# A fused attention and feed-forward block on Trainium2: taking out the filler matmuls of the attention stage and issuing each diagonal chunk last

## What is computed

```python
xn = layernorm(x)
q, k, v = xn @ Wq.T, xn @ Wk.T, xn @ Wv.T        # 16, 16, 64 features per head
qf, kf = taylor_exp(q), taylor_exp(k)            # [1, x/2, (x outer x)/(sqrt(2)*4)]
A = tril(einsum('bhnd,bhmd->bhnm', qf, kf))
y = einsum('bhnm,bhme->bhne', A, v)
y = y * rsqrt(mean(y*y) + 1e-5) * g_weight       # per token and head
attn = y @ Wo.T
h = gelu(einsum('bsd,fd->bsf', xn, ternary(W1)) + b1)
ffn = einsum('bsf,df->bsd', h, ternary(W2)) + b2
out = x + attn + ffn
```

## Time and profile before

| what | us |
|---|---|
| median of 2 runs | 1793.25 (1790.44 and 1796.06) |
| profiled execution | 1789.8 |
| its span on the slowest core (core 4) | 1787.9 |
| spans of the eight cores | 1754.8 to 1787.9 |

### The profile page before, as it was taken

How to read it: one execution, slowest core, us unless ns; L and a number is a source line. 1 busy time by engine, 2 the same in 40 slices (tenths; PEclk the granted TensorE clock), 3 DMA queues, 4 the chain that set the end, 5 groups by cost and what they waited for, 6 DMA issues and landing times.

```text
span 1787.9 us, 16908 instructions; the slowest of 8 cores (1754.8 to 1787.9 us)
## 1 busy us (share of the span) xinstructions
PE 1266.6 (71%) x4584; PEld 438.1 (25%) x4584; DVE 569.5 (32%) x1295; ACT 532.9 (30%) x886; POOL 93.1 (5%) x155
## 2 busy tenths in 40 slices
PE   0000296798979797989978872937888881499996
PEld 0000043122222222212222221313333330244442
DVE  2222007644343444334354443443222220000100
ACT  1553332344333444324444432212233330000000
POOL 1111000000000000000000000001111110000000
PEclk9999698686555777656668685968999996699998
DMA  8889905000010101010001016844445446465662
GB/s 190 258 262 219 175 1 94 7 8 11 1 18 0 18 1 30 1 30 1 14 16 30 1 24 153 299 168 147 158 153 158 159 156 191 126 163 138 153 163 48
DMA packets 154328, 176.24 MB, mean 99 GB/s; under 512 B 73856, under 2 KB 125056, under 8 KB 150144
## 3 DMA queue, kind: packets, MB, share of 16 engines
q0 software_dynamic: 24928, 97.53, 19.7%
q1 hardware_dynamic: 129312, 77.63, 17.3%
HBM read 119.56 MB, written 41.94 MB: 90 GB/s over the span
## 4 chain that ended last, share of the span: by engine, by line
PE 49%; DMA 30%; DVE 10%; issue 6%; SPq 2%; ACT 1%; POOL 1%; DVEq 0%; POOLq 0%; ACTq 0%
PE psY L726 12%; PE psY L711 11%; DMA wst<-w2T 9%; PE psS L758 9%; PE psS L833 6%; DMA p1st<-w1T 5%; PE psS L705 4%; DMA xnT<-xn_tm 4%; DMA hg_ts<-hg_scr 4%; DMA w_sb<-w2t_scr 3%; PE psY L833 2%; DMA y_tm<-y_pair 2%; PE psS L797 2%; PE psY L797 2%; DVE jw2a L551 1%
## 5 line engine op out<-in xcount | busy, mean ns | idle before, releaser
L639 ACT ACTIVATE A_buf<-psS,consts 128x512 bf16<-128x512 f32 (+3 forms) x427 | 282.2, 711 | 456.5 <-PE psS L758 455.3
L758 PE MATMUL psS<-qh_ext,kh_ext 16*128 16x512 bf16 (+3 forms) x640 | 216.9, 427 | 109.9 <-DVE A_buf L460 83.4
L811 PE MATMUL psS<-xnT,w_sb 128*128 128x512 bf16 x1024 | 230.0, 383 | 76.9 <-DVE w_sb L515 39.4
L711 PE MATMUL psY<-v_tm,zlhs 128*128 128x512 bf16 x512 | 247.6, 484 | 0.0
L726 PE MATMUL psY<-A_buf,v_tm 128*64 128x512 bf16 (+3 forms) x640 | 235.4, 482 | 0.0
L456 DVE TENSOR_SCALAR pv<-psS 128x512 bf16<-128x512 f32 (+3 forms) x213 | 129.6, 608 | 261.1 <-PE psS L758 251.7
L705 PE MATMUL psS<-xnT,wq_bf 128*128 128x512 bf16 x64 | 21.2, 504 | 207.8 <-DMA xnT<-xn_tm 207.8
L833 PE MATMUL psS<-w_sb,hg_ts 128*128 128x512 bf16 x512 | 113.6, 383 | 64.6 <-DMA hg_ts<-hg_scr 64.4
L811 PEld LDWEIGHTS psS<-xnT,w_sb 128*128 128x128 bf16 x1024 | 98.3, 98 | 208.4 <-issue 98.3
L672 ACT ACTIVATE hgst<-psS,consts 128x512 bf16<-128x512 f32 x128 | 84.9, 685 | 178.5 <-DMA hg_scr<-hgst 108.5
L833 PE MATMUL psY<-w_sb,hg_ts 128*128 128x512 bf16 x512 | 111.8, 379 | 0.0
(11 more groups left out here) (96 smaller groups left out, 738.2 us busy)
## 6 DMA issues: line engine op xcount, KB each, us to landing
p1st<-w1T POOLq DMA_DIRECT2D x16, 1024.0 KB, 7.5
p1st<-w2T POOLq DMA_DIRECT2D x16, 1024.0 KB, 8.5
wst<-w1T POOLq DMA_DIRECT2D x16, 1024.0 KB, 8.4
wst<-w2T POOLq DMA_DIRECT2D x32, 512.0 KB, 4.8
hg_scr<-hgst SPq DMA_DIRECT2D x128, 128.0 KB, 2.7
hg_ts<-hg_scr SPq DMA_DIRECT2D x32, 512.0 KB, 7.8
x_roll<-x SPq DMA_DIRECT2D x16, 512.0 KB, 6.1
out<-out_sb SPq DMA_DIRECT2D x16, 512.0 KB, 5.0
```

Source lines behind the costliest of these rows:

```text
L639: e.activation(A_buf[:, gs % 4, t0:t0 + w], psS[idx % 4][:, 0:w], AF.Square, bias=cc(C_CBI), scale=cc(C_CSC)).then_inc(sPOLY, 1)
L711: e.matmul(psY[:, 1536:2048], zlhs[:], v_tm[:, 0, 0:512], start=False, stop=False)
L758: e.matmul(psS[idx % 4][:, 0:w], kh_ext[:, hi, m * 128:(m + 1) * 128], qh_ext[:, hi, t0:t0 + w], start=True, stop=True).then_inc(sSC, 1)
L811: mm = e.matmul(ps[:], w12_sb[:, c * FF + j * 128:c * FF + j * 128 + 128], xnT[:, 4 * tb:4 * tb + 4, c, :], start=(c == 0), stop=(c == KD ...
```

## The change

```diff
@@ -715,7 +715,9 @@
             chs = strip_chunks(m)
             for hi, h in ((0, 2 * p), (1, 2 * p + 1)):
                 gs = strip_of[(p, m, hi)]
-                for ci, (t0, w) in enumerate(chs):
+                order = list(range(1, len(chs))) + [0]
+                for ci in order:
+                    t0, w = chs[ci]
                     idx = poly_idx[(p, m, hi, ci)]
                     if ci == 0:
                         e.wait_ge(sDM, dm_of[(p, m, hi)] + 1)
@@ -728,7 +730,6 @@
                              A_buf[:, gs % 4, t0:t0 + w],
                              start=False, stop=False)
                 e.sem_inc(sAV, 1)
-                dummy_mm(e)
 
         def close_b(e, p, b):
```

## The result

The changed kernel takes 1594.0 us (median of 11 runs, 1584.4 to 1621.4). The kernel before, run beside it, takes 1789.0. The ratio is 0.893, with a 95% interval of 0.889 to 0.897: 10.7% faster. Medians and ranges here are of all runs; ratios and comparisons leave out runs such as the one of 1621.4, in which one die took longer at a lower clock.

What follows compares the result with a forecast made beforehand. TensorE was taken to bound the attention stage by its streaming and clock. 318.4 + 617 (pairs of 77.7) + 739.8, less 3.3 tail and 16 clock return, gave 1656; profiling and median offsets made 1661 us, range 1600 to 1710.

Steps and rivals of the forecast that it cites:

- The wait at a pair's head: TensorE's wait for the transpose and VectorE's normalizing: 9.2 us, plus 0.7 us without the first filler.
- the check: Attention stage: ScalarE and VectorE can keep up with 77.7 us a pair; four score buffers cover ScalarE's 0.7 us lag.
- The later stages: Everything after the last score, taken as untouched: 739.8 us carried over for core 6, expected to be slowest.
- The chunk order: Diagonal chunk last in AV strips: wins nothing where filler covered the mask, now a guard; put at 0.
- rival 3: Attention blocks: filler hid a wait for the mask before AV; 25 us a pair, 1880 us, slower; chance 0.04.
- A switch between scores and AV: Two per block stay, 32 a pair, at 0.13 us each: 4.2 us a pair (0 to 8).
- rival 2: Attention stage: only the filler's streaming comes free, each switch keeps its 0.25 us; 16 us a pair, 1771 us; chance 0.10.
- Rival 1: Blocks 5 to 12: the clock holds high, saving 12 us a pair; 1581, or 1595 with misses; chance 0.24.
- the sum: One attention pair at 1.2 GHz throughout: 61.4 + 4.2 + 9.2 + 0.7 + 2.2 = 77.7 us.
- streaming that stays: AV as many: Attention pair: scores 34,816 columns, AV as many, plus 8 matmuls of 512: 73,728 columns, 61.4 us.
- the return of the clock: Two clock lifts a pair after AV in blocks 0 to 3, about 1 us each: 16 us off the time.
- The wait at a pair's tail: After a pair's last score: of five fillers' 3.3 us only 1.1 comes off, 2.2 turns into waiting.

Runs made afterwards that it cites:

- experiment 1: Changed kernel with head 1's AV matmuls writing to the same 64 PSUM partitions as head 0's, no instruction added or removed: 1671.2 us, ratio to before 0.933.
- Experiments 1 and 2: The second: changed kernel plus one matmul of zeros, 128 wide and 16 columns long, between the two heads' AV strips: 1702.1 us, ratio 0.951.

## Why the prediction was right and where it failed

**Right.** TensorE sets the pace; the filler stood on its path; without it the clock stays low throughout (0.50 in the stage, the granted clock of every slice) and the kernel is faster all the same. The cores came closer, 25 us apart (1564.2 to 1588.9) instead of 33. The wait at a pair's head was 9.8 us in the mean of the eight on core 1 (7.2 to 11.2), where the account had 9.2 + 0.7. ScalarE and VectorE kept up as the check said: outside the heads of pairs the scores waited for VectorE 9.8 us in the whole stage, where it was 10.9 before, and no longer for ScalarE. The later stages were not changed by the edit, but they are not as steady as I took them: the slowest core was core 1, with 731.6 us, and core 6, which I had expected to be slowest with 739.8, needed 722.1 and was the fastest. The chunk order won nothing, and AV waits for the mask 5.7 us in all, which ends rival 3. A switch between scores and AV costs about what I took: in experiment 1 eight AV matmuls hold TensorE 3.55 us for 3.41 of streaming, 0.14 for 0.13 taken, so rival 2 is gone as well. Rival 1, the clock held in the middle blocks, named nearly the right time (1595) by luck, for a wrong reason: no block of the stage ran at the higher level.

**Where it failed: the first term of the sum, "streaming that stays: AV as many".** I let the 34,816 AV columns of a pair stream one after the other, because they did so before, in the rows of the trace. But each row of AV before ended at a filler, and the trace could not show what two heads do side by side. It should have been a bound from both sides: 29 us if they queue, 14.5 if they run together. The code said so, `psY[64 * hi:64 * hi + 64]`, and I left the change from strip to strip out of the switches, which puts it at 0 and never below. Experiments 1 and 2 settle it: without the overlap AV takes 88 us more and the kernel 77, and a separator of 16 columns undoes it.

**The sum with the measured terms.** 1661 less 8 x 14.5 = 116 for a full overlap gives 1545. Add 16 for the return of the clock, which did not come: with AV stretches of 1.9 us it stayed at 0.50, where with those of 3.5 us in experiment 1 it rose at times. That makes 1561, 33 us under the measured time, and the trace of core 1 shows where they are:

- The overlap is not full. From the first start of an AV stretch to the next scores, all stretches together take 148 us, where half of the streaming is 116: the second head's matmuls start up to 0.3 us behind the first's (411.92 and 411.63) and end as much later. The scores take 29 us more than their streaming of 232. Against these 61 us the sum had 8 x 4.2 = 33.6 for switches: about 28 us short.
- Waits: 538 - 435.4 = 102.6 us, where the sum had 8 x 9.9 + 7 x 2.2 = 94.6. The wait at a pair's tail was 0.8 us instead of 2.2, but waits for VectorE outside the pair's head (9.8 us) and of AV for the mask (5.7 us) stood at nothing in the sum: 8 us short.
- Outside the stage: the start and the tail of the last pair 5 us more, the later stages 8 us less than the 739.8 carried over.

**The range** ended at 1600 since its low end leaned on the clock alone. A bound for the overlap would have put it at about 1545, and the measured time inside.

## What to carry to other kernels

A matmul that fills time between others can also separate them: before counting only its columns, look at which rows and columns of the array the neighbours use, and whether they could run side by side without it. A filler that is to hold the clock must be weighed against both costs, its columns and the lost overlap; here it bought a mean clock of 0.69 instead of 0.50 and cost more than it gave. When an edit removes an instruction between two others, bound the pair from both sides, as the trace of before can't show them adjacent.

## What the runs showed of the hardware that I had not expected

- Matmuls on different column halves, in program order head 0's four and then head 1's four, still overlap: eight in 1.88 us. The two need not alternate in the program: in all 72 AV stretches of the stage where the last matmul of a strip is a narrower one, head 1's wide ones start before head 0's narrow one.
- A separator of 16 columns that itself takes 0.12 us costs 108 us over 128 places.
- Contraction of 16 rows on different row groups overlaps too: four 512-wide score matmuls in about half the time (1.03 us busy against 1.88, both at 0.50).
- A busy TensorE alone does not lift the clock: it stood at 0.50 throughout the stage in the changed kernel and in the run with filler on the scores only, where TensorE was busy 552 of 630 us.
